# Moving three small operations of a threshold search from VectorE to GpSimd, and reordering ScalarE, in a sparse-attention block

## The chip, the cores and the metric

One core of one Trainium2 chip. The metric is the device time of one execution in microseconds, median of several. TensorE is PE in the profile's rows, VectorE is DVE, ScalarE is ACT, GpSimd is POOL.

## The reference, cut to what matters

A transformer block on x of shape (16, 512, 128): attention with 16 heads of 64 and 16 memory keys per head, whose scores are mixed across heads, cut to each row's 64 largest, and whose probabilities are mixed across heads again; then a gated feed-forward layer (384 hidden). Both are wrapped in layer norms and residuals.

```python
q, k, v = split_heads(x @ Wq), split_heads(x @ Wk), split_heads(x @ Wv)
k, v = concat([mem_k, k]), concat([mem_v, v])
dots = einsum('bhij,hk->bkij', einsum('bhid,bhjd->bhij', q, k) * scale, pre_proj)
dots = where(causal, neg, dots)
vk = top_k(dots, 64)[0][..., -1:]
attn = softmax(where(dots < vk, neg, dots))
out = einsum('bhij,bhjd->bhid', einsum('bhij,hk->bkij', attn, post_proj), v)
```

## The kernel before, in words

The weights are folded once at the start, so that a head's scores are one product of x' with a 128x512 matrix. Then come 16 batches of 16 heads: 256 heads, one **step** per head and a few steps to drain. Batches 1 to 14 run in a loop over b, two batches per turn, with the 16 steps written out. Each engine has its own program; they meet by semaphores alone. The 512 queries of a head stand as four tiles t of 128 rows with 144, 272, 400 and 528 columns (keys up to the diagonal and 16 memory keys); `ORDER` is 3, 2, 1, 0.

In step s the engines work on several heads at once, at lags of 0 to 7 steps:

- **Score** (lag 0): TensorE makes the scores (L760), VectorE copies them out with the row maximum (L1209). GpSimd places the memory scores (L1332) and, a step later, the negative maximum `negmax` (L1317).
- **Guess** (lags 1 to 3): the 64th largest score of each row is searched for. Three rounds, three heads at a time: ScalarE counts by a Sign activation with its sum (L915, twelve in a step) how many scores lie above a guess, and VectorE makes the next guess by a secant or bracket step out of a chain of small instructions, 12 or 24 columns wide, each of which waits for the one before: L1122 `miss`, L1123 `between`, L1127 `product`, L1130, L1134, L1138, L1140, L1142 (reciprocal), L1143, L1145, L1148 (the new guesses, `guess_ready`).
- **Select** (`LAG_K`, 4): VectorE counts the scores at or above the last guess (L1075, `count_found`, sum in `found`), GpSimd subtracts (L1357, four instructions), which hides them from the eight-largest search.
- **Check** (`LAG_E`, 5): VectorE tests (L1104 `spread`, L1109 `missed`) whether the count was within a window; TensorE adds the flags over the rows (L749, `raise_flag`), VectorE copies them out of PSUM between two L1209 (L1072, `copy_flag`). A missed tile gets a general search (L1042 to L1050). ScalarE makes the exponentials (L936).
- **Apply** (`LAG_P`, 6): VectorE takes the eight largest of the rest (L1089, four MAX8). GpSimd's `offset` (L1338) gives the rank that each would have, L1092 picks the one of rank 64 and L1097 adds it up to `kth`. Then VectorE masks and sums the probabilities (L1190, four) and takes the reciprocal `rinv` (L1195); GpSimd makes four diagonals of it (L1349) and `pmem` (L1363); TensorE turns and scales the blocks by them (L784), ScalarE takes them out of PSUM (L926).
- **Values** (`LAG_V`, 7): TensorE adds up the output (L771).

VectorE's order in a step: MAX8, L1092, L1097, L1104, L1109, the guess chain, L1075 of tile 3, a feed-forward pair (L1164, L1170; steps 11 to 13), L1075 of tile 2, L1190 four times, L1195, L1075 of tiles 1 and 0, L1209 four times. At its end stand the statistics of a norm (L1010, L1015; steps 0, 7, 8, 14) or the memory maxima (L1030, step 10).

GpSimd's order: negmax, seed copy (L1323), memory copy, offset, then in steps 1, 8, 9 and 15 a norm (L1258, L1261, L1265 for x, L1270) and in 8 and 15 a residual (L1276, L1277), the diagonals, the subtractions, pmem.

TensorE's order: scores, a piece of other work, weighing, the next head's matrix G, the flag, the turned blocks, other work. In step 7 the memory part of the output (L738) stands ahead of the weighing. ScalarE's order: counts, other copies, turned block 0, G (L846), block 1, exponential of tile 3, block 2, the other exponentials, other copies.

`alone` (L281) is a nop that carries an instruction's waits, so that the instruction itself has none.

## Time and profile before

| | us |
|---|---|
| median of 3 runs | 3318.77 (3317.39 to 3321.68) |
| the profiled execution | 3324.22 |
| its span, first to last instruction | 3322.4 |
| busy: VectorE | 2884.4 (87%) |
| ScalarE | 2882.6 (87%) |
| TensorE matmuls | 2794.6 (84%) |
| GpSimd | 1737.9 (52%) |

The granted TensorE clock is 0.954 of full speed on average. DMA is nearly idle: 7 GB/s. Busy time counts instructions of the engine and not its waits, nops and semaphore instructions; instructions of one engine may overlap by some 0.05 to 0.1 us, so that the start of one and the start of the next are what adds up. The profile's page gives shares over the whole span; for a change inside the step the timelines of a single step say more, and these are read below.

### The profile page before, as it was taken

How to read it: one execution, taken by the hardware profiler on the slowest of the kernel's cores; microseconds unless marked ns; L12 is line 12 of the kernel's file. 1: busy time of each engine (PE TensorE's matmuls, PEld its weight loads, DVE VectorE, ACT ScalarE, POOL GpSimd, SP SyncE). 2: the span in 40 equal slices, each digit the busy share in tenths (PEclk: the TensorE clock that was granted, in tenths of full speed). 3: DMA queues.
4: the chain of work that ended last, by engine and by line, in shares of the span. 5: the costliest groups of instructions: out<-in, count | busy, mean ns of one | idle time of the engine just before them, and what ended most of it. 6: DMA issues, size and time to landing. Idle time of an engine off the chain costs nothing. (4 is left out here: it accounts for less than half of the span.)

```text
span 3322.4 us, 76028 instructions
## 1 busy us (share of the span) xinstructions
PE 2794.6 (84%) x16314; PEld 2046.5 (62%) x16314; DVE 2884.4 (87%) x12547; ACT 2882.6 (87%) x8666; POOL 1737.9 (52%) x3623
## 2 busy tenths in 40 slices
PE   6888888888878888888898878888788898888865
PEld 3466666666656666666666656666566666666654
DVE  4599888989989899998889989989889889998884
ACT  1699899998978989899898979989899898989972
POOL 3355555555545555555555545545555555555543
PEclk9999999999989999999999989999999999999987
DMA  1000000000000000000000000000000000000000
GB/s 45 7 2 2 5 8 5 9 2 5 9 5 9 2 12 2 5 9 5 9 2 12 2 5 8 2 12 2 5 9 5 9 2 12 2 5 9 2 8 4
DMA packets 31421, 22.93 MB, mean 7 GB/s; under 512 B 3201, under 2 KB 30338, under 8 KB 30722
## 3 DMA queue, kind: packets, MB, share of 16 engines
q1 hardware_dynamic: 30722, 16.03, 1.7%
q14 instruction: 555, 4.55, 0.5%
q8 instruction: 144, 2.36, 0.3%
HBM read 11.83 MB, written 4.19 MB: 5 GB/s over the span
## 5 line engine op out<-in xcount | busy, mean ns | idle before, releaser
L915 ACT ACTIVATE signs<-scores,state 128x528 int8<-128x528 f32 (+3 forms) x3072 | 1726.3, 585 | 40.5 <-DVE state L1148 40.0
L784 PE MATMUL t_bank<-diag,probs 128*128 128x128 f32 x5120 | 760.9, 308 | 453.8 <-POOL diag L1349 400.5
L1349 POOL TENSOR_SCALAR diag<-ident,rinv 128x128 f32<-128x128 f32 x1024 | 362.2, 374 | 1360.1 <-DVE rinv L1195 1360.1
L784 PEld LDWEIGHTS t_bank<-diag,probs 128*128 128x128 f32 x5120 | 694.2, 216 | 494.1 <-issue 359.1
L1357 POOL TENSOR_TENSOR work<-scores,work 128x528 f32<-128x528 f32 (+3 forms) x1024 | 889.0, 903 | 10.8 <-DVE work L1075 10.8
L760 PE MATMUL s_bank<-xn,gT 128*128 128x512 f32 (+3 forms) x2048 | 685.7, 457 | 0.9 <-ACT gT L846 0.7
L771 PEld LDWEIGHTS y_bank<-u_all,probsT 128*128 128x128 f32 x5120 | 609.0, 192 | 107.3 <-issue 98.9
L915 ACT ACTIVATION_READ_ACCUMULATOR signs<-scores,state 128x1 f32 x3072 | 646.5, 210 | 0.0
L926 ACT COPY probsT<-t_bank 128x512 f32<-128x512 f32 (+1 forms) x768 | 406.9, 530 | 266.3 <-PE t_bank L784 265.1
L771 PE MATMUL y_bank<-u_all,probsT 128*128 128x128 f32 x5120 | 617.3, 276 | 5.3 <-ACT probsT L926 5.3
L1075 DVE TENSOR_SCALAR_CACHE_REDUCE work<-scores,state 128x528 f32<-128x528 f32 (+3 forms) x1024 | 531.1, 553 | 46.2 <-DVE state L1148 46.2
L936 ACT ACTIVATE expo<-scores,negmax 128x528 f32<-128x528 f32 (+3 forms) x1024 | 546.7, 599 | 0.0
L1190 DVE SCALAR_TENSOR_TENSOR probs<-scores,kth,expo 128x528 f32<-128x528 f32 (+3 forms) x1024 | 525.5, 569 | 12.3 <-ACT expo L936 5.8
L1209 DVE TENSOR_SCALAR_CACHE_REDUCE scores<-s_bank,memmax 128x512 f32<-128x512 f32 (+3 forms) x1024 | 516.7, 543 | 6.0 <-PE s_bank L762 6.0
L760 PEld LDWEIGHTS s_bank<-xn,gT 128*128 128x128 f32 x2048 | 326.5, 193 | 227.9 <-issue 220.5
L1089 DVE MAX8 state<-work 128x8 f32<-128x528 f32 (+3 forms) x1024 | 441.6, 491 | 0.2 <-issue 0.2
L632 PE MATMUL misc<-b_all,xn 128*128 128x512 f32 x512 | 273.4, 616 | 7.5 <-ACT u_all L846 7.5
L669 PE MATMUL misc<-xn,a_all 128*128 128x512 f32 x512 | 262.5, 594 | 0.0
L762 PE MATMUL s_bank<-causal,ident 128*128 128x128 bf16 x1024 | 224.6, 219 | 0.0
L762 PEld LDWEIGHTS s_bank<-causal,ident 128*128 128x128 bf16 x1024 | 101.1, 99 | 103.3 <-issue 63.2
L846 ACT COPY u_all<-misc 128x512 f32<-128x512 f32 x256 | 151.4, 591 | 7.0 <-PE misc L632 7.0
L846 ACT COPY gT<-misc 128x512 f32<-128x512 f32 x256 | 154.2, 602 | 0.9 <-PE misc L669 0.9
(156 smaller groups left out, 2846.5 us busy)
## 6 DMA issues: line engine op xcount, KB each, us to landing
xwork<-in_L_attn_x_dram SPq DMA_DIRECT2D x17, 256.0 KB, 2.8
xres<-in_L_attn_x_dram SPq DMA_DIRECT2D x16, 256.0 KB, 2.9
out_dram<-ybuf SPq DMA_DIRECT2D x16, 256.0 KB, 2.4
u_all<-in_L_attn_Wq_dram SPq DMA_DIRECT2D x1, 512.0 KB, 3.6
u_all<-in_L_attn_Wk_dram SPq DMA_DIRECT2D x1, 512.0 KB, 4.5
u_all<-in_L_attn_Wv_dram SPq DMA_DIRECT2D x1, 512.0 KB, 5.5
u_all<-in_L_attn_Wo_dram SPq DMA_DIRECT2D x1, 512.0 KB
expo<-in_L_ffn_w_gate_dram SPq DMA_DIRECT2D x1, 192.0 KB, 4.7
```

Of the source, the lines that this page charges most:

```text
L760: nc.tensor.matmul(score_part(t, 0, KEYS[t]), lhsT=gT[s % 2][:, t * P:(t + 1) * P], rhs=xn[par][:, 0:KEYS[t]], start=True, stop=False, ski ...
L771: mm = nc.tensor.matmul(y_bank[:, t * P:(t + 1) * P], lhsT=probsT[:, h % 2, at:at + P], rhs=u_all[:, j, h * D:(h + 1) * D], start=False, s ...
L784: mm = nc.tensor.matmul(t_bank[q % 2][:, at:at + P], lhsT=probs[:, h % 2, KEY_AT[t] + j * P:KEY_AT[t] + (j + 1) * P], rhs=diag[:, t, :], s ...
L915: nc.scalar.activation(signs[:, k, AT[t]:AT[t] + ROW[t]], row(scores, ring(head_of(s, k + 1), RING), t), ACT.Sign, bias=guesses(s % STATES ...
L926: nc.scalar.copy(probsT[:, h % 2, PART_AT[q]:PART_AT[q + 1]], t_bank[q % 2][:, 0:PART_AT[q + 1] - PART_AT[q]]).then_inc(t_taken, 1)
L936: nc.scalar.activation(row(expo, ring(head_of(s, LAG_E), ERING), t), row(scores, ring(head_of(s, LAG_E), RING), t), ACT.Exp, bias=negmax[: ...
L1075: v.tensor_scalar(work[:, s % 2, AT[t]:AT[t] + ROW[t]], row(scores, slot_k, t), guessed[:, t:t + 1], None, ALU.is_ge, ALU.add, accum_out=f ...
L1089: v.max(candidates(past)[:, t, 1:9], work[:, s % 2, AT[t]:AT[t] + ROW[t]]).then_inc(select_step, 1)
L1190: v.scalar_tensor_tensor(out=probs[:, slot_p % 2, AT[t]:AT[t] + ROW[t]], in0=row(scores, slot_p, t), scalar=kth[:, bass.ds(slot_p, 1), t], ...
L1209: v.tensor_scalar(keys(scores, slot, t), score_part(t, 0, KEYS[t]), 1.0, memmax[par][:, t, bass.ds(s, 1)], ALU.mult, ALU.max, accum_out=ro ...
L1349: nc.gpsimd.tensor_scalar(diag[:, t, :], ident[:, :], rinv[:, slot_p, t:t + 1], 1.0, ALU.mult, ALU.mult).then_inc(scaled, 1)
L1357: nc.gpsimd.tensor_tensor(wrk, row(scores, slot_k, t), wrk, ALU.subtract).then_inc(hidden, 1)
```

## The change

- **GpSimd tests missed rows, a step ahead.** The constants of L1338 get two more columns a tile, so that one addition of `found` gives the two distances from the window's ends too; `spread` is their product (a tensor_tensor of 128x4), `missed` a comparison (tensor_scalar). Both, and `offset`, now run at `LAG_K`, behind the diagonals and ahead of the subtractions. `offset` and `missed` get two buffers. VectorE's L1104 and L1109 go. The sum over the tiles, which L1109 made by its accumulator, is made by `copy_flag`, now a tensor_scalar with an accumulator.
- **TensorE** makes the flag right behind the scores, and no longer behind weighing and G.
- **`between` (L1123)** moves to GpSimd, a step ahead, behind the norms and ahead of the diagonals; it waits for the guess of its own step. VectorE's L1130 waits for it.
- **The pick** (L1092, L1097) moves from ahead of the guess chain into it: the rank weighing stands behind L1145, ahead of L1148, the sum behind L1148.
- **The count of tile 2** moves between the two feed-forward products L1164 and L1170.
- **ScalarE** takes G and the exponentials of tiles 3 and 2 ahead of turned block 0, then blocks 0 and 1, exponential 1, block 2, exponential 0.

```diff
@@ -137,11 +137,13 @@
             active = n + M > TOPK
             table[i, t] = z * UNIT ** 0.5
             table[i, T + t] = (z - FAR / (2 * density)) * UNIT ** 0.5
-            table[i, 5 * T + 9 * T + t] = float(active)
-            table[i, 5 * T + 10 * T + t] = 0.0 if active else -FMAX
+            reach = WINDOW + 0.5 if active else FAR
+            table[i, 5 * T + 11 * t] = reach - AIM
+            table[i, 5 * T + 11 * t + 1] = -reach - AIM
+            table[i, 5 * T + 11 * T + t] = 0.0 if active else -FMAX
         for k in range(GUESSES):
             table[:, 2 * T + k * T + t] = ROW[t] - 2 * AIM - 0.25
-        table[:, 5 * T + 9 * t:5 * T + 9 * t + 9] = np.arange(9) - TOPK
+        table[:, 5 * T + 11 * t + 2:5 * T + 11 * t + 11] = np.arange(9) - TOPK
     return table
 
 
...
@@ -791,6 +795,8 @@
                     g = b * H + s
                     if kind != "drain":
                         score(kind, b, par, s, g)
+                    if lagged(kind, s, LAG_E):
+                        raise_flag(kind, g - LAG_E, head_of(s, LAG_E) % 2)
                     make_extra(kind, b, par, s, 0)
                     if s == LAG_V and kind != "first":
                         memory_y(kind, b)
@@ -801,8 +807,6 @@
                         weigh(head_of(s, LAG_V), g - LAG_V)
                     if makes_g(kind, s):
                         product_g(kind, b, par, par if s < H - 1 else 1 - par, s + 1)
-                    if lagged(kind, s, LAG_E):
-                        raise_flag(kind, g - LAG_E)
                     if lagged(kind, s, LAG_P):
                         for q in range(3):
                             turn(head_of(s, LAG_P), g - LAG_P, q)
@@ -947,14 +951,15 @@
                     count(2)
                     count(1)
                     take_extra(0)
-                    take_turned(0)
                     if makes_g(kind, s):
                         take(kind, b, par, ("G", s + 1), gT[(s + 1) % 2][:, :])
+                    exponentials(0)
+                    exponentials(1)
+                    take_turned(0)
                     take_turned(1)
-                    exponentials(0)
+                    exponentials(2)
                     take_turned(2)
-                    for p in range(1, T):
-                        exponentials(p)
+                    exponentials(3)
                     take_extra(1)
 
                 for s in range(H):
@@ -1053,7 +1058,7 @@
 
             dve.wait_ge(table_in, 16)
             dve.wait_ge(state_set, 3)
-            nc.vector.tensor_copy(offset[:, :, 9:10].squeeze(2), cap)
+            nc.vector.tensor_copy(offset[:, :, :, 11:12].squeeze(3), cap.unsqueeze(1).to_broadcast([P, 2, T]))
 
             def batch(kind, b, par):
                 def step(s):
@@ -1069,12 +1074,26 @@
 
                         dve.wait_ge(flag_full, ge + 1)
                         alone(dve)
-                        v.tensor_copy(flags[:, :], flag_part).then_inc(flag_taken, 1)
+                        v.tensor_scalar(flags[:, 0:T], flag_part, 1.0, None, ALU.mult, ALU.add,
+                                        accum_out=flags[:, T:T + 1]).then_inc(flag_taken, 1)
 
                     def count_found(t):
                         v.tensor_scalar(work[:, s % 2, AT[t]:AT[t] + ROW[t]], row(scores, slot_k, t), guessed[:, t:t + 1],
                                         None, ALU.is_ge, ALU.add,
                                         accum_out=found[:, s % 2, t:t + 1]).then_inc(found_ready, 1)
+
+                    def weigh_ranks():
+                        dve.wait_ge(offset_ready, gp + 1)
+                        dve.wait_ge(select_step, T)
+                        v.scalar_tensor_tensor(out=offset[:, slot_p % 2, :, 2:11], in0=offset[:, slot_p % 2, :, 2:11], scalar=0.0,
+                                               in1=candidates(past), op0=ALU.is_equal,
+                                               op1=ALU.mult).then_inc(select_step, 1)
+
+                    def pick():
+                        dve.wait_ge(select_step, T + 1)
+                        dve.sem_clear(select_step)
+                        v.tensor_reduce(kth[:, bass.ds(slot_p, 1), :].squeeze(1), offset[:, slot_p % 2, :, 2:12], AX_X,
+                                        ALU.add).then_inc(kth_ready, 1)
 
                     if applies:
 
@@ -1087,28 +1106,6 @@
                                 rows_missed = dve.value_load(flags[0:1, T:T + 1].bitcast(I32), min_val=0,
                                                              max_val=2 ** 31 - 1)
                             v.max(candidates(past)[:, t, 1:9], work[:, s % 2, AT[t]:AT[t] + ROW[t]]).then_inc(select_step, 1)
-                        dve.wait_ge(offset_ready, gp + 1)
-                        dve.wait_ge(select_step, T + 1)
-                        v.scalar_tensor_tensor(out=offset[:, :, 0:9], in0=offset[:, :, 0:9], scalar=0.0,
-                                               in1=candidates(past), op0=ALU.is_equal,
-                                               op1=ALU.mult).then_inc(select_step, 1)
-                        dve.wait_ge(select_step, T + 2)
-                        dve.sem_clear(select_step)
-                        v.tensor_reduce(kth[:, bass.ds(slot_p, 1), :].squeeze(1), offset[:, :, :], AX_X,
-                                        ALU.add).then_inc(kth_ready, 1)
-
-                    if checks:
-                        number = found[:, (s - 1) % 2, :]
-                        dve.wait_ge(found_ready, 4 * ge + 4)
-                        alone(dve)
-                        v.scalar_tensor_tensor(out=spread[:, :], in0=number, scalar=-2.0 * AIM, in1=number,
-                                               op0=ALU.add, op1=ALU.mult).then_inc(select_step, 1)
-                        dve.wait_ge(select_step, 1)
-                        at_least(dve, flag_full, ge)
-                        alone(dve)
-                        v.scalar_tensor_tensor(out=missed[:, 0:T], in0=spread[:, :], scalar=WINDOW ** 2 + 0.5 - AIM ** 2,
-                                               in1=active, op0=ALU.is_gt, op1=ALU.mult,
-                                               accum_out=missed[:, T:T + 1]).then_inc(bad_ready, 1)
 
                     if moves:
                         for k in range(GUESSES):
@@ -1120,13 +1117,13 @@
                         miss = pair(last, S_T, 0)[:, 1]
                         both, last_at = last_and_now(last)
                         v.tensor_tensor(miss, counts[:, (s - 1) % 2, :], aim_sum, ALU.subtract).then_inc(guess_step, 1)
-                        v.tensor_tensor(between[:, :, :], pair(past, S_T, -1), pair(last, S_OTHER, 0),
-                                        ALU.subtract).then_inc(guess_step, 1)
                         dve.wait_ge(guess_step, 1)
 
                         v.tensor_tensor(product[:, :, :], both, miss.unsqueeze(1).to_broadcast([P, 2, ALL]),
                                         ALU.mult).then_inc(guess_step, 1)
-                        dve.wait_ge(guess_step, 3)
+                        dve.wait_ge(guess_step, 2)
+                        dve.wait_ge(between_ready, g - 1)
+                        alone(dve)
                         v.scalar_tensor_tensor(out=between[:, :, :],
                                                in0=product[:, last_at, :].unsqueeze(1).to_broadcast([P, 2, ALL]),
                                                scalar=0.0, in1=between[:, :, :], op0=ALU.is_lt,
@@ -1134,18 +1131,25 @@
                         v.scalar_tensor_tensor(out=move[:, :], in0=product[:, 1 - last_at, :],
                                                scalar=(2 * WINDOW + 0.25) ** 2 + 1.0,
                                                in1=miss, op0=ALU.is_gt, op1=ALU.mult).then_inc(guess_step, 1)
-                        dve.wait_ge(guess_step, 4)
+                        dve.wait_ge(guess_step, 3)
                         v.tensor_tensor(other, pair(last, S_OTHER, 0), between[:, :, :], ALU.add).then_inc(guess_step, 1)
+                        dve.wait_ge(guess_step, 5)
+                        v.tensor_tensor(apart[:, :, :], pair(last, S_T, 0), other, ALU.subtract).then_inc(guess_step, 1)
                         dve.wait_ge(guess_step, 6)
-                        v.tensor_tensor(apart[:, :, :], pair(last, S_T, 0), other, ALU.subtract).then_inc(guess_step, 1)
-                        dve.wait_ge(guess_step, 7)
                         v.reciprocal(apart[:, 1, :], apart[:, 1, :]).then_inc(guess_step, 1)
                         v.tensor_tensor(move[:, :], apart[:, 0, :], move[:, :], ALU.mult).then_inc(guess_step, 1)
+                        dve.wait_ge(guess_step, 8)
+                        v.tensor_tensor(move[:, :], move[:, :], apart[:, 1, :], ALU.mult).then_inc(guess_step, 1)
                         dve.wait_ge(guess_step, 9)
-                        v.tensor_tensor(move[:, :], move[:, :], apart[:, 1, :], ALU.mult).then_inc(guess_step, 1)
-                        dve.wait_ge(guess_step, 10)
                         dve.sem_clear(guess_step)
+                        if applies:
+                            weigh_ranks()
                         v.tensor_tensor(guesses(now, 1, GUESSES), guess, move[:, :], ALU.subtract).then_inc(guess_ready, 1)
+
+                    if applies:
+                        if not moves:
+                            weigh_ranks()
+                        pick()
 
                     if selects:
                         guessed = guesses(now, GUESSES, 1)
@@ -1164,13 +1168,15 @@
                         v.scalar_tensor_tensor(out=f_up[:, c, :], in0=f_tanh[:, c, :], scalar=1.0,
                                                in1=misc[gate_at][:, :], op0=ALU.add, op1=ALU.mult
                                                ).then_inc(misc_free[gate_at], 1)
+
+                    if selects:
+                        count_found(ORDER[1])
+
+                    if 11 <= s < 11 + HC and kind != "first":
                         dve.wait_ge(misc_free[gate_at], turns_of_bank(kind, b, misc_at(kind, ("GATE", c))) + 1)
                         dve.wait_ge(misc_full, misc_index(kind, b, ("UP", c)) + 1)
                         alone(dve)
                         v.tensor_tensor(f_up[:, c, :], f_up[:, c, :], misc[up_at][:, :], ALU.mult).then_inc(misc_free[up_at], 1)
-
-                    if selects:
-                        count_found(ORDER[1])
 
                     if applies:
                         at_least(dve, t_full, 3 * (gp - 1))
@@ -1331,14 +1337,14 @@
                         alone(pool)
                         nc.gpsimd.tensor_copy(mem_parts(scores[:, bass.ds(slot, 1), :].squeeze(1)),
                                               head_mem(smem[par], s)).then_inc(mem_placed, 1)
-                    if lagged(kind, s, LAG_E):
-                        at_least(pool, kth_ready, g - LAG_E)
-                        pool.wait_ge(found_ready, 4 * (g - LAG_E) + 4)
+                    extras(kind, b, s)
+                    moves_next = any(lagged(kind, s + 1, k + 2) for k in range(GUESSES)) if s + 1 < H else kind != "drain"
+                    if moves_next:
+                        at_least(pool, guess_ready, g - 1)
+                        at_least(pool, first_ready, g if kind != "drain" or s == 0 else 0)
                         alone(pool)
-                        nc.gpsimd.tensor_tensor(offset[:, :, 0:9], ranks,
-                                                found[:, (s - 1) % 2, :].unsqueeze(2).to_broadcast([P, T, 9]),
-                                                ALU.add).then_inc(offset_ready, 1)
-                    extras(kind, b, s)
+                        nc.gpsimd.tensor_tensor(between[:, :, :], pair((s - 1) % STATES, S_T, -1), pair(s % STATES, S_OTHER, 0),
+                                                ALU.subtract).then_inc(between_ready, 1)
                     gp, slot_p = g - LAG_P, head_of(s, LAG_P) % 2
                     if lagged(kind, s, LAG_P):
                         pool.wait_ge(rinv_ready, gp + 1)
@@ -1350,6 +1356,22 @@
                                                     ALU.mult).then_inc(scaled, 1)
                     if lagged(kind, s, LAG_K):
                         gk, slot_k = g - LAG_K, ring(head_of(s, LAG_K), RING)
+                        ranked = offset[:, slot_k % 2, :, :]
+                        at_least(pool, kth_ready, gk - 1)
+                        pool.wait_ge(found_ready, 4 * gk + 4)
+                        alone(pool)
+                        nc.gpsimd.tensor_tensor(ranked[:, :, 0:11], ranks,
+                                                found[:, s % 2, :].unsqueeze(2).to_broadcast([P, T, 11]),
+                                                ALU.add).then_inc(offset_ready, 1)
+                        pool.wait_ge(offset_ready, gk + 1)
+                        alone(pool)
+                        nc.gpsimd.tensor_tensor(spread[:, :], ranked[:, :, 0:1].squeeze(2), ranked[:, :, 1:2].squeeze(2),
+                                                ALU.mult).then_inc(spread_ready, 1)
+                        pool.wait_ge(spread_ready, gk + 1)
+                        at_least(pool, flag_full, gk - 1)
+                        alone(pool)
+                        nc.gpsimd.tensor_scalar(missed[:, slot_k % 2, :], spread[:, :], 0.0, 1.0, ALU.is_gt,
+                                                ALU.mult).then_inc(bad_ready, 1)
                         for p, t in enumerate(ORDER):
                             pool.wait_ge(found_ready, 4 * gk + p + 1)
                             alone(pool)
```

## Rows read from the trace of the kernel before

**Rows 1.** Windows: a plain step, then sixteen steps; us and instructions of each engine, clock, DMA.
```profile
core 0: us, PE busy (x) PEld busy (x) DVE busy (x) ACT busy (x) POOL busy (x), PEclk, DMA share, GB/s
1500.99:1512.05 11.06, 10.06 (x61) 7.13 (x60) 10.10 (x46) 11.06 (x35) 5.81 (x13) 1.00 0.00 1
1538.17:1733.60 195.43, 170.47 (x1008) 126.23 (x1007) 175.48 (x775) 179.08 (x541) 106.73 (x226) 0.96 0.02 6
```

**Rows 2.** Waits: who waited for whom; us in total, times, longest.
```profile
DVE flags L1072 <- issue: 20.4, 16, 2.6
...
DVE f_up L1170 <- DVE f_up L1164: 5.9, 30, 0.2
```

**Rows 3.** Timeline of VectorE in a plain step: start us, us, what.
```profile
1504.64 0.18 DVE L1195 RECIPROCAL rinv<-rowsum 128x4 f32<-128x4 f32 x1
...
1507.37 1.73 DVE L1089 MAX8 state<-work 128x8 f32<-128x528 f32 x4
1509.21 0.33 DVE L1092 SCALAR_TENSOR_TENSOR offset<-offset,state 128x36 f32<-128x36 f32 x1
...
1510.37 0.17 DVE L1122 TENSOR_TENSOR state<-counts,consts 128x12 f32<-128x12 f32 x1
...
1510.80 0.18 DVE L1130 SCALAR_TENSOR_TENSOR between<-product,between 128x24 f32<-128x24 f32 x1
...
1511.75 0.17 DVE L1145 TENSOR_TENSOR move<-move,apart 128x12 f32<-128x12 f32 x1
...
1512.39 0.76 DVE L1075 TENSOR_SCALAR_CACHE_REDUCE work<-scores,state 128x528 f32<-128x528 f32 x1 [0.17 <-DVE state L1148]
```

**Rows 4.** Timeline of GpSimd in the same step, asked in short windows.
```profile
1506.45 1.31 POOL L1357 TENSOR_TENSOR work<-scores,work 128x528 f32<-128x528 f32 x1
...
1507.71 1.04 POOL L1357 TENSOR_TENSOR work<-scores,work 128x400 f32<-128x400 f32 x1
...
1508.70 0.76 POOL L1357 TENSOR_TENSOR work<-scores,work 128x272 f32<-128x272 f32 x1
...
1509.42 0.49 POOL L1357 TENSOR_TENSOR work<-scores,work 128x144 f32<-128x144 f32 x1
1509.87 0.30 POOL L1363 TENSOR_TENSOR pmem<-probs,rinv 128x64 f32<-128x64 f32 x1
1510.12 0.21 POOL L1317 TENSOR_TENSOR negmax<-rowmax,minus_unit 128x4 f32<-128x4 f32 x1
...
1510.39 0.25 POOL L1332 COPY scores<-smem 128x64 f32<-128x64 f32 x1
```

**Rows 5.** Timeline of VectorE and GpSimd in one of the last steps.
```profile
3244.49 0.58 DVE L1109 SCALAR_TENSOR_TENSOR missed<-spread,consts 128x4 f32<-128x4 f32 x1
...
3245.01 0.53 DVE L1122 TENSOR_TENSOR state<-counts,consts 128x12 f32<-128x12 f32 x1
...
3242.04 3.47 POOL L1357 TENSOR_TENSOR work<-scores,work 128x528 f32<-128x528 f32 x4
```

**Rows 6.** Timeline of both engines while GpSimd normalises x (step 1).
```profile
1649.96 1.04 POOL L1261 TENSOR_TENSOR rstd<-vareps,minus_half 128x4 f32<-128x4 f32 x1
...
1650.23 0.18 DVE L1138 TENSOR_TENSOR state<-state,between 128x24 f32<-128x24 f32 x1
...
1651.14 1.04 POOL L1265 TENSOR_TENSOR xwork<-xwork,meanvar 128x512 f32<-128x512 f32 x1
1651.26 0.95 DVE L1148 TENSOR_TENSOR state<-state,move 128x12 f32<-128x12 f32 x1
```

**Rows 7.** Timeline of both engines while GpSimd adds the residual (step 8).
```profile
1539.75 0.96 DVE L1190 SCALAR_TENSOR_TENSOR probs<-scores,kth,expo 128x528 f32<-128x528 f32 x1
1540.10 1.19 POOL L1277 TENSOR_TENSOR xres<-xres,ybuf 128x256 f32<-128x256 f32 x1
...
1540.64 1.09 DVE L1190 SCALAR_TENSOR_TENSOR probs<-scores,kth,expo 128x400 f32<-128x400 f32 x1
```

**Rows 8.** Timeline of VectorE at the end of step 7.
```profile
1532.19 0.85 DVE L1010 BATCH_NORM_STATS2 stats<-ybuf 128x6 f32<-128x128 f32 x4
...
1533.47 1.71 DVE L1089 MAX8 state<-work 128x8 f32<-128x528 f32 x4
```

20 lines of the change are left out of this document (11 added, 9 removed).

## The prediction

> **What bounds the kernel now.** I read the windows first. In a plain step (one without norm statistics, maxima or feed-forward work on VectorE) ScalarE is busy for all of 11.06 us and VectorE for 10.10; over sixteen steps, 195.43 us, ScalarE has 16.4 us to spare, VectorE 19.9, GpSimd 88.7 [rows 1]. The timeline of VectorE then shows that its spare time is latency: it goes straight from one small dependent instruction to the next, and starts the next head's count when the guess is done [rows 3]. It hardly waits for others; the waits name a flag (20.4 us in 16 places) and the feed-forward products (5.9 us) [rows 2]. So VectorE's own chain sets the step, 12.2 us on average, and ScalarE with 179.08/16 = 11.2 us of work is the next limit, 1.0 us below.
>
> Times from here count from the end of L1195 (1504.82 in rows 3). MAX8 runs from 2.55 to 4.28 (four instructions; the next small one, L1092, starts at 4.39), L1122 at 5.55, L1130 at 5.98, L1145 at 6.93, the first count L1075 at 7.57 [rows 3]. GpSimd, which also starts from L1195, subtracts in four pieces from 1.63 to 5.10, then pmem to 5.35, negmax, seed and memory copy to 5.83 [rows 4]. Both orders hang on the same instruction, so their phase repeats in every step.
>
> **What is removed.** L1092 to L1122 is 1.16 us of rank weighing, sum, spread and missed; all leaves this place. L1123 was issued in the latency of L1122 and saves nothing. If nothing came in its way, L1122 would start at 4.25 (its waits are met, and it need not wait for MAX8's result), 1.3 us sooner.
>
> **What comes in.** L1130 gets a second wait and a nop, 0.1 us. Behind L1145 stand the rank weighing and, behind L1148, the sum: L1145 to L1075 is 0.64 us now [rows 3]; with up to 0.33 for the one and 0.2 for the other and their waits I take 1.0 (bounds 0.75 and 1.15). The flag's copy gets an accumulator read, which overlaps the next L1209: nothing, at most 0.1. Without other effects a step gains 1.3 - 0.1 - 0.36 = 0.85 us.
>
> **Where it collides.** GpSimd gets three small instructions between the diagonals and the subtractions. Their kind takes 0.21 to 0.25 us (negmax, the memory copy [rows 4]), and one that depends on the one before starts 0.14 behind its end (L1261 to L1265 [rows 6]): 0.25 + 0.14 + 0.21 + 0.14 + 0.23 = 0.97 us (bounds 0.7 and 1.1). The pieces now start at 2.60, 3.86, 4.85 and 5.57 and end at 3.91, 4.90, 5.61 and 6.06; pmem ends at 6.31, negmax at 6.47, the memory copy at 6.78. VectorE's guess chain has two operands in SBUF nearly throughout, and the rows show what happens to such an instruction under a GpSimd one: in the last steps L1122, 0.17 us in rows 3, took 0.53, and L1109 ahead of it 0.58; their ends, 3245.07 and 3245.54, are 0.02 to 0.03 behind the ends of the third piece and of the last one (3245.51) [rows 5]. L1148 took 0.95, to 0.03 behind the end of L1265 [rows 6]. GpSimd's pieces kept their pace.
>
> So in a plain step after the change: L1122 starts at 4.3 and ends with the second piece, 4.92; the product starts 0.04 later, under the third piece, ends 5.65; L1130 ends with the fourth, 6.10; L1134 with pmem, 6.35; L1138 with negmax, 6.51; L1140 with the memory copy, 6.82. L1142 follows at 6.86, L1145 at 7.15, L1075 at 8.15 against 7.57: **0.58 us slower**, where the free chain would be 0.85 faster. Five of sixteen steps are clean like this (+2.9 us); six more have waits of their own for instructions or registers that partly overlap the block; I estimate +0.25 each, between nothing and 0.58 (+1.5 us).
>
> In five steps VectorE does 1.1 to 1.3 us of other work ahead of MAX8 (L1010 to the next MAX8 is 1.28 [rows 8]). MAX8 then ends near 5.55 and only the product meets a full piece. L1075 starts at about 8.2. Before it was 5.55 + 3.29 = 8.84, and in four of the five (steps 1, 8, 9, 15; 52 times in the trace, all like the one shown) L1148 was caught by a norm's pass, 0.95 for 0.17, another 0.78 [rows 6]: 9.6. These passes now start at about 8.33, and L1148 at 7.75, so it is through. Gains 1.3 at steps 9, 15, 1.1 at 1 and 0.4 at 11. Step 8 gains 1.3 and also 1.1 of the flag's wait, as TensorE makes the flag ahead of the long weighing and not behind it: 20.4/16 = 1.28 [rows 2]. But L1190 comes earlier into GpSimd's residual and centring passes: the engines then take turns, as they do in some steps now, L1190 0.96 and then, with fewer elements, 1.09, and L1277 1.19 [rows 7]. Each turn costs VectorE what is left of a pass, 0.2 to 0.6. I charge 0.8 at steps 1, 8 and 15 (bounds 0 and 1.2), less 0.3 at 8, where every second batch pays it now. Net for steps 9, 15, 1, 8, 11: -1.3 - 0.5 - 0.3 - 1.9 - 0.4 = -4.4 us.
>
> A count between the two feed-forward products hides their 0.1 us latency and wait, three times: -0.4 us. **ScalarE's new order** I cost at nothing: it fills waits with work, but nobody waits for ScalarE; what covers it is VectorE's 12.2 us step, and if that fell under 11.2 it would be worth what ScalarE idles. GpSimd's `between` runs beside L1075, which has one SBUF operand, and is due 8 us later: nothing; if GpSimd were late there, the diagonals behind it would be.
>
> **Sum.** 2.9 + 1.5 - 4.4 - 0.4 = -0.4 us in sixteen steps, 16 batches: -6. The profiled execution took 3324.2 (span 3322.4), so 3318; the median shown is 5.4 lower, so **3312 us**. The gain from the shorter chain is real and is eaten by the collision.
>
> One row decides a further term. L1261 ran from 1649.96 to 1651.00, and L1138 inside it took 0.18, as L1130 does alone [rows 3, 6], so I let the power instruction block nobody. If it did block, as L1265 does, L1145 would wait for its end in four steps of a batch and its successors would meet the norm behind it: 0.8 + 0.8 = 1.6 us each, 16 x 4 x 1.6 = 100 us, 3412. The Trainium skill (SBUF — State Buffer, Who interferes with whom) says that a VectorE instruction with two SBUF inputs and a GpSimd one that reads SBUF exclude each other for the whole instruction, which would be this case; the trace agrees for the subtractions and norms, and disagrees for L1261.
>
> **Rivals.**
> 1. The chain is hardly caught (my phase is wrong, or the first small instruction slips in and the rest follow). Each step gains 0.85, plus the L1148 blocks and the flag: 16 x 0.85 + 4 x 0.78 + 1.3 = 18 us in a batch; ScalarE's work (179.08 us a batch [rows 1]) and its remaining waits cap that at 8 to 12: 3125 to 3190 us. Against it: no instruction slipped through [rows 5]. For it: the phase is put together from small durations. 0.15.
> 2. **Slower:** the late steps gain less than I count. If L1148 starts later than 8.3 (0.5 behind my 7.75), the norm's pass catches it again: 0.78 in four steps, 3.1 us a batch; with 0.58 in all eleven plain steps instead of seven's worth (another 2.0), +4.7 us a batch, 3394 us. It decides from a chain 0.5 us longer than mine, or a GpSimd shift of 0.7 or less that brings the norms forward. For it: the margins are a few tenths. 0.2.
> 3. The power instruction blocks too, as worked out above, 3412 us: L1138 speaks against it [rows 6]. 0.03.
> 4. The forecast, 3312, within 3270 to 3355: 0.62. It is the difference of two terms of 70 and 77 us, so its sign is open: about half of it is faster, a fifth within 0.2% (7 us, about what a measurement of this kernel can tell from no change), the rest slower.
>
> Faster: 0.15 + 0.31 = 0.46; same 0.12; slower 0.2 + 0.03 + 0.19 = 0.42. The range leaves out rivals 1 and 3 and little more: 3220 to 3395.
>
> **What would show it.** In a plain step: L1122, the product, L1130, L1134 of 0.3 to 0.7 us each, ending 0.02 to 0.04 behind L1357's pieces and pmem, and L1075 8.15 behind L1195 (rival 1: 6.7). The first L1357 at 2.6. L1148's longest duration: 0.17 as I say, 0.95 for rival 2. No wait in front of the flag's copy at step 7. L1190 and L1277 stretched at 1, 8 and 15. ScalarE's wait for turned blocks nearly gone, without a gain in time. I am wrong if VectorE's small instructions keep 0.17 us while the subtractions run, or if VectorE waits for ScalarE's counts.

## The result, and the profile of the changed kernel

The changed kernel takes **3371.24 us** (median of 4 runs, 3367.18 to 3372.79) against 3320.11 for the kernel before: ratio 1.0152, 95% interval 1.0136 to 1.0168. It is slower by 51 us, where I forecast 3312. One run of the woven version in experiment 6 took 5454.96 us against 3241 to 3248 of its other three, which alone have a median of 3242.86; its median, ratio and interval below count that run. The profiled execution has a span of 3365.2 us at a mean granted clock of 0.962; the one before had 3322.4.

The windows of a plain step and of sixteen steps, with the columns of [rows 1]:

```profile
1528.34:1539.96 11.62, 10.20 (x63) 7.21 (x62) 11.01 (x45) 11.45 (x35) 6.45 (x16) 1.00 0.01 2
1565.37:1761.74 196.37, 169.82 (x1005) 123.54 (x1006) 183.37 (x729) 180.14 (x537) 119.21 (x273) 0.97 0.02 6
```

VectorE is busy for 11.01 of 11.62 us where it was for 10.10 of 11.06, with one instruction fewer (45 for 46). So its instructions got longer. The timeline of VectorE in a plain step, which answers to [rows 3]:

```profile
1909.53 0.18 DVE L1201 RECIPROCAL rinv<-rowsum 128x4 f32<-128x4 f32 x1
...
1912.27 1.73 DVE L1108 MAX8 state<-work 128x8 f32<-128x528 f32 x4
1913.92 0.74 DVE L1119 TENSOR_TENSOR state<-counts,consts 128x12 f32<-128x12 f32 x1
1914.69 0.69 DVE L1122 TENSOR_TENSOR product<-state 128x24 f32<-128x24 f32 x1
1915.52 0.31 DVE L1127 SCALAR_TENSOR_TENSOR between<-product,between 128x24 f32<-128x24 f32 x1
1915.76 0.32 DVE L1131 SCALAR_TENSOR_TENSOR move<-product,state 128x12 f32<-128x12 f32 x1
1915.99 0.24 DVE L1135 TENSOR_TENSOR state<-state,between 128x24 f32<-128x24 f32 x1
1916.27 0.27 DVE L1137 TENSOR_TENSOR apart<-state 128x24 f32<-128x24 f32 x1
...
1916.86 0.17 DVE L1142 TENSOR_TENSOR move<-move,apart 128x12 f32<-128x12 f32 x1
1917.24 0.22 DVE L1088 SCALAR_TENSOR_TENSOR offset<-offset,state 128x36 f32<-128x36 f32 x1 [0.21 <-DVE move L1142]
1917.38 0.17 DVE L1147 TENSOR_TENSOR state<-state,move 128x12 f32<-128x12 f32 x1
1917.60 0.20 DVE L1095 TENSOR_REDUCE kth<-offset 128x4 f32<-128x40 f32 x1
1917.83 0.76 DVE L1081 TENSOR_SCALAR_CACHE_REDUCE work<-scores,state 128x528 f32<-128x528 f32 x1
```

and GpSimd in the same step, which answers to [rows 4] (a row now holds the four pieces):

```profile
1911.34 0.26 POOL L1363 TENSOR_TENSOR offset<-consts,found 128x44 f32<-128x44 f32 x1
1911.74 0.20 POOL L1368 TENSOR_TENSOR spread<-offset 128x4 f32<-128x4 f32 x1
1912.13 0.24 POOL L1373 TENSOR_SCALAR missed<-spread 128x4 f32<-128x4 f32 x1 [0.19 <-POOL spread L1368]
1912.33 3.46 POOL L1379 TENSOR_TENSOR work<-scores,work 128x528 f32<-128x528 f32 x4
1915.75 0.29 POOL L1385 TENSOR_TENSOR pmem<-probs,rinv 128x64 f32<-128x64 f32 x1
1916.00 0.20 POOL L1323 TENSOR_TENSOR negmax<-rowmax,minus_unit 128x4 f32<-128x4 f32 x1
...
1916.27 0.24 POOL L1338 COPY scores<-smem 128x64 f32<-128x64 f32 x1
```

Count again from the reciprocal's end, 1909.71. The three tests take 1911.34 to 1912.33, so the subtractions start at 2.62 instead of 1.63 and end at 6.08. The first small instruction behind MAX8 (L1119) starts at 4.21 and takes 0.74 us, the product 0.69. The next four end at 1915.83, 1916.08, 1916.23 and 1916.54, and GpSimd's last piece, pmem, negmax and memory copy at 1915.79, 1916.04, 1916.20 and 1916.51: each is held to 0.03 or 0.04 us behind one of them. The first count (L1081) starts at 8.12; it was 7.57.

The waits of VectorE, which answer to [rows 2]:

```profile
DVE offset L1088 <- DVE move L1142: 60.9, 254, 0.6
DVE probs L1196 <- issue: 33.7, 46, 3.5
...
DVE f_up L1179 <- PE misc L732: 0.4, 1, 0.4
```

The flag (20.4 us before) and the latency of the feed-forward products (5.9) are gone, as forecast. A wait of "issue" in front of `probs` is new: 33.7 us in 46 places. Before it was 5.6 in 3: 3.5 us in a step that ran the general search, 1.9 where the loop ends and 0.2 at the end of the program. It is the second half of the story. In step 9 of every second batch:

```profile
1967.24 0.76 DVE L1081 TENSOR_SCALAR_CACHE_REDUCE work<-scores,state 128x528 f32<-128x528 f32 x1
...
1967.93 0.63 DVE L1081 TENSOR_SCALAR_CACHE_REDUCE work<-scores,state 128x400 f32<-128x400 f32 x1
...
1969.41 0.77 DVE L1196 SCALAR_TENSOR_TENSOR probs<-scores,kth,expo 128x528 f32<-128x528 f32 x1 [0.85 <-issue]
```

ScalarE had ended the exponentials of that head 6 us earlier:

```profile
1962.66 0.42 ACT L940 ACTIVATE expo<-scores,negmax 128x144 f32<-128x144 f32 x1
```

Between the second count and `probs` VectorE's sequencer passes a conditional branch (L1187, in the kernel before L1181), past the general search for rows whose candidates don't suffice. In most steps the next instruction of the sequencer follows the branch 0.51 us later, which the second count covers; in four places of the loop's 32 steps (steps 7 and 9 of one batch, 4 and 15 of the other), 1.2 to 1.8 us later. In a fifth, step 0, that instruction is in time and `probs` behind it is late.

I split steps 16 to 255 of both traces at four instructions; after less before, sums in us: reciprocal to the end of MAX8 -18.6; MAX8 to the first count +8.4 (plain steps +76, the five long ones -68); first count to `probs` +21.0; `probs` to the reciprocal +29.9. Together +40.8. The long steps are 1, 8, 9, 11 and 15, in which VectorE does other work ahead of MAX8.

The last section holds the turns that the prediction names: VectorE's L1196 and GpSimd's residual hold each other up, at steps 1, 8 and 15. In step 8 (400 columns take 0.63 us in a plain step):

```profile
1562.89 1.09 DVE L1196 SCALAR_TENSOR_TENSOR probs<-scores,kth,expo 128x400 f32<-128x400 f32 x1
```

```profile
1562.27 1.27 POOL L1282 TENSOR_TENSOR xres<-xres,ybuf 128x256 f32<-128x256 f32 x1
```

### The profile page after: what moved, and what is told of

Same layout as the page of the kernel before. It is cut to its first block and busy times, and to the rows that moved or that the text cites. A ratio compares the mean times of both kernels' runs of the same rounds, so it can differ in the third digit from the quotient of the medians.

```text
span 3365.2 us, 76754 instructions
## 1 busy us (share of the span) xinstructions
PE 2815.9 (84%) x16314; PEld 2023.6 (60%) x16314; DVE 3015.9 (90%) x11777; ACT 2912.6 (87%) x8666; POOL 1937.2 (58%) x4393
## 5 line engine op out<-in xcount | busy, mean ns | idle before, releaser
L788 PE MATMUL t_bank<-diag,probs 128*128 128x128 f32 x5120 | 746.9, 301 | 476.6 <-POOL diag L1355 372.5
L788 PEld LDWEIGHTS t_bank<-diag,probs 128*128 128x128 f32 x5120 | 671.5, 208 | 702.7 <-issue 525.3
L1196 DVE SCALAR_TENSOR_TENSOR probs<-scores,kth,expo 128x528 f32<-128x528 f32 (+3 forms) x1024 | 555.2, 597 | 39.4 <-issue 33.4
L919 ACT ACTIVATION_READ_ACCUMULATOR signs<-scores,state 128x1 f32 x3072 | 581.8, 189 | 0.0
L940 ACT ACTIVATE expo<-scores,negmax 128x528 f32<-128x528 f32 (+3 forms) x1024 | 564.5, 577 | 0.0
L1081 DVE TENSOR_SCALAR_CACHE_REDUCE work<-scores,state 128x528 f32<-128x528 f32 (+3 forms) x1024 | 531.1, 553 | 16.4 <-issue 3.6
L930 ACT COPY probsT<-t_bank 128x512 f32<-128x512 f32 (+1 forms) x768 | 376.3, 510 | 179.6 <-PE t_bank L788 177.7
L636 PE MATMUL misc<-b_all,xn 128*128 128x512 f32 x512 | 281.1, 631 | 7.5 <-ACT u_all L850 7.5
L1346 POOL TENSOR_TENSOR between<-state 128x24 f32<-128x24 f32 x258 | 74.5, 289 | 262.1 <-DVE state L1147 262.1
L1122 DVE TENSOR_TENSOR product<-state 128x24 f32<-128x24 f32 x258 | 157.1, 609 | 9.0 <-DVE state L1119 0.2
```

Of the source, the lines that this page charges most:

```text
L788: mm = nc.tensor.matmul(t_bank[q % 2][:, at:at + P], lhsT=probs[:, h % 2, KEY_AT[t] + j * P:KEY_AT[t] + (j + 1) * P], rhs=diag[:, t, :], s ...
L919: nc.scalar.activation(signs[:, k, AT[t]:AT[t] + ROW[t]], row(scores, ring(head_of(s, k + 1), RING), t), ACT.Sign, bias=guesses(s % STATES ...
L930: nc.scalar.copy(probsT[:, h % 2, PART_AT[q]:PART_AT[q + 1]], t_bank[q % 2][:, 0:PART_AT[q + 1] - PART_AT[q]]).then_inc(t_taken, 1)
L940: nc.scalar.activation(row(expo, ring(head_of(s, LAG_E), ERING), t), row(scores, ring(head_of(s, LAG_E), RING), t), ACT.Exp, bias=negmax[: ...
L1081: v.tensor_scalar(work[:, s % 2, AT[t]:AT[t] + ROW[t]], row(scores, slot_k, t), guessed[:, t:t + 1], None, ALU.is_ge, ALU.add, accum_out=f ...
L1196: v.scalar_tensor_tensor(out=probs[:, slot_p % 2, AT[t]:AT[t] + ROW[t]], in0=row(scores, slot_p, t), scalar=kth[:, bass.ds(slot_p, 1), t], ...
```

## The experiments

The kernel before took 3319 to 3324 us (medians) beside them. Ratios are to it, with their intervals.

**1. The flag alone**, in the kernel before:

```diff
                         score(kind, b, par, s, g)
+                    if lagged(kind, s, LAG_E):
+                        raise_flag(kind, g - LAG_E)
                     make_extra(kind, b, par, s, 0)
...
-                    if lagged(kind, s, LAG_E):
-                        raise_flag(kind, g - LAG_E)
```

> The kernel before, with only TensorE's flag product moved to right behind the scores. If the wait of VectorE in front of the flag's copy at step 7 (20.4 us in 16 places before, none after the change) is on the path, this alone gives the 18.6 us that the section from L1195 to the end of MAX8 gained in the changed kernel: 3300 us, ratio 0.994. Rival: the wait only moves (to the statistics behind it or to ScalarE's counts): ratio 1.000.

3304.81 us, 0.994 (0.9923 to 0.9956). The section ahead of MAX8's end loses 21.0 us, 19.6 of it at step 8. The flag is worth what the prediction gave it.

**2. ScalarE's order alone**, in the kernel before (the order of the diff above, nothing else):

> The kernel before, with only ScalarE's new order. As VectorE's chain sets the step and waits for ScalarE hardly anywhere, I expect ratio 1.000 within 0.001 and ScalarE's wait for turned blocks much reduced. Rival: ScalarE's order brings its exponentials of tiles 1 and 0 later or its counts earlier, and shows in the time: ratio 0.99 or 1.01.

3345.08 us, 1.0067 (1.005 to 1.0084), **not** nothing. The wait for the flag has grown from 20.4 us [rows 2] to 45.2; the row of that kernel's waits:

```profile
DVE flags L1073 <- issue: 45.2, 18, 5.2
```

**3. Both together**, in the kernel before, if the order costs only through the late flag:

> The kernel before with two parts of the change, the flag's matmul right behind the scores and ScalarE's new order. Theory (ScalarE's order cost 22 us alone because it made TensorE's late flag later still; with the early flag nobody waits for it): 0.994 of the kernel before, the same as the early flag alone, 3300 to 3310 us. Rival (the order costs VectorE something by itself): 1.000 or above.

3310.79 us, 0.9974 (0.9964 to 0.9984): between the two. Of the 20.7 us that the order cost ahead of MAX8's end, 1.7 are left, as the theory has it, so the two parts are not independent. But the time is just above my range. What stays, 0.0034 or about 11 us over the flag alone, is nearly all another wait, again for TensorE, in the feed-forward steps (8.1 us at step 11). In the kernel before it was 4.6 us, with the flag alone 6.7; with the flag and the order:

```profile
DVE f_up L1171 <- PE misc L728: 18.0, 24, 1.4
```

**4. The changed kernel with the old order of ScalarE:**

> The changed kernel with ScalarE's order of the kernel before. Theory (as in the prediction, the order is hidden in this kernel: VectorE waits 0.4 us in all for the UP product): 3365 to 3377 us, the same as the changed kernel. Rival (the order costs here too, as it did alone): 3340 to 3360 us.

3378.1 us, 1.0182 (1.0166 to 1.0198), 1 us above my range and 7 us above the changed kernel's 1.0152. There the new order is free, even of some use; VectorE waits 0.4 us in all for that product.

**5. The subtractions taken away** from the changed kernel:

```diff
-  nc.gpsimd.tensor_tensor(wrk, row(scores, slot_k, t), wrk, ALU.subtract).then_inc(hidden, 1)
+  nc.gpsimd.tensor_tensor(wrk[:, 0:1], row(scores, slot_k, t)[:, 0:1], wrk[:, 0:1],
+                          ALU.subtract).then_inc(hidden, 1)
...
-  v.max(candidates(past)[:, t, 1:9], work[:, s % 2, AT[t]:AT[t] + ROW[t]]).then_inc(select_step, 1)
+  v.max(candidates(past)[:, t, 1:9], row(scores, slot_p, t)).then_inc(select_step, 1)
```

It leaves out the hiding of the keys above the guess (one column is still subtracted), and MAX8 reads the scores as they are.

> The changed kernel with GpSimd's four subtractions cut to one column each, and MAX8 reading the scores themselves, so that it does as much work as ever; left out is the hiding of the scores above the guess, so the threshold is another one. Collision theory: with the subtractions gone VectorE's guess chain runs freely, L1122, product, L1130 and L1134 fall to 0.17 to 0.2 us, L1075 starts near 6.8 instead of 8.13 behind L1195, and ScalarE (11.2 us a step) becomes the limit: 3150 to 3230 us. Rival (the chain's own latency and instruction supply make the loss): 3340 or more.

3233.02 us, 0.9733 (0.9717 to 0.9749), 138 us under the changed kernel and 3 us above my range. The chain in a step without other work of VectorE:

```profile
1824.16 1.73 DVE L1108 MAX8 state<-scores 128x8 f32<-128x528 f32 x4
1826.79 0.17 DVE L1119 TENSOR_TENSOR state<-counts,consts 128x12 f32<-128x12 f32 x1 [0.90 <-issue]
1826.99 0.18 DVE L1122 TENSOR_TENSOR product<-state 128x24 f32<-128x24 f32 x1
1827.32 0.18 DVE L1127 SCALAR_TENSOR_TENSOR between<-product,between 128x24 f32<-128x24 f32 x1
1827.42 0.17 DVE L1131 SCALAR_TENSOR_TENSOR move<-product,state 128x12 f32<-128x12 f32 x1
1827.54 0.18 DVE L1135 TENSOR_TENSOR state<-state,between 128x24 f32<-128x24 f32 x1
```

Every small instruction is at its own length. In plain steps where nothing else is waited for, the first count starts at 6.61 to 6.70 behind the reciprocal, the 6.7 of rival 1. But with VectorE this fast L1119 waits in steps 5 to 8 for ScalarE's counts (0.90 us here; the last count ended at 1826.70), and in steps 1, 8 and 15 the norm's passes now lie over the update, so that the first count comes at 9.2 to 10.4 (means of the steps). That is why not every step gains 1.5 us.

**6. The tests a step later.** GpSimd's three tests stand behind the memory copy, outside the stretch of the subtractions; once with the pick whole, ahead of the guess update, once woven in as in the change:

```diff
                         nc.gpsimd.tensor_copy(mem_parts(...), head_mem(smem[par], s)).then_inc(mem_placed, 1)
+                    if lagged(kind, s, LAG_E):
+                        ge = g - LAG_E
...
+                        nc.gpsimd.tensor_tensor(ranked[:, :, 0:11], ranks, ...).then_inc(offset_ready, 1)
...
+                        nc.gpsimd.tensor_tensor(spread[:, :], ...).then_inc(spread_ready, 1)
...
+                        nc.gpsimd.tensor_scalar(missed[:, par_e, :], ...).then_inc(bad_ready, 1)
                     extras(kind, b, s)
```

> The changed kernel, with GpSimd's three tests (offset, spread, missed) done a step later, behind the memory copy and so outside the subtractions' time, and the pick whole again, ahead of the guess update. Theory (the cost of the change is the later start of the subtractions, which then lie over the guess update): the first subtraction starts 1.63 us behind the reciprocal again, the first count of the next head 7.1 us behind it in a plain step (8.13 after the change, 7.57 before), 0.9 to 1.1 us less than after the change in eleven steps; 3215 to 3260 us, faster than both kernels. Rival (the weaving, or ScalarE's order, costs the time, or work moved anywhere on GpSimd costs VectorE as much): within 10 us of the changed kernel or above it.

> The same placing of GpSimd's tests, with the pick woven into the guess update as in the change. Theory: the product and its neighbours meet the subtractions' last piece, one instruction of latency is saved by the weaving; first count at 7.2 to 7.3 us, 3220 to 3270 us, within 15 us of the unwoven one. Rival (weaving is worth most of the gain, or costs it): the two differ by over 25 us.

Unwoven 3264.47 us, 0.9837 (0.9817 to 0.9856), 4 us above my range; its first count is at 7.4 in most plain steps, 0.7 us ahead of the changed kernel's, where I expected 0.9 to 1.1. Woven 3245.18 us, 0.9778 (0.9758 to 0.9797). The two differ by 19 us, 22 without the long run, which is neither my theory (within 15) nor the rival (over 25). A step of the woven one:

```profile
1837.22 0.48 DVE L1119 TENSOR_TENSOR state<-counts,consts 128x12 f32<-128x12 f32 x1
1837.73 0.43 DVE L1122 TENSOR_TENSOR product<-state 128x24 f32<-128x24 f32 x1
1838.30 0.19 DVE L1127 SCALAR_TENSOR_TENSOR between<-product,between 128x24 f32<-128x24 f32 x1
...
1840.30 0.76 DVE L1081 TENSOR_SCALAR_CACHE_REDUCE work<-scores,state 128x528 f32<-128x528 f32 x1
```

Counted from its reciprocal (1833.01), the first count is at 7.29, 0.83 ahead of the changed kernel's 8.12. That is 12 to 14 us over the trace for each of the eleven plain steps of a batch, and 124 us in the span. **One microsecond of phase on GpSimd decides the sign of this change.** The three instructions cost GpSimd the same in both versions; only what they push differs.

**7. The changed kernel with the pick unwoven** (tests where the change puts them):

```diff
+                        weigh_ranks()
+                        pick()
                     if moves:
...
-                        if applies:
-                            weigh_ranks()
...
-                    if applies:
-                        if not moves:
-                            weigh_ranks()
-                        pick()
```

> The changed kernel with the pick whole again, ahead of the guess update, and GpSimd's tests where the change puts them. Theory (in plain steps the guess update is paced by the subtractions' ends in either order, so the pick is hidden when it stands ahead, and lies bare behind the update when woven in): first count 0.2 to 0.3 us earlier in plain steps, 0.3 later in the five long ones; 3335 to 3365 us. Rival (the pick adds its whole length ahead of the update): 3385 us or above.

3328.74 us, 1.0035 (1.0022 to 1.0048), 42 us under the changed kernel and below my range.

```profile
1887.88 0.60 DVE L1088 SCALAR_TENSOR_TENSOR offset<-offset,state 128x36 f32<-128x36 f32 x1
1888.61 0.20 DVE L1095 TENSOR_REDUCE kth<-offset 128x4 f32<-128x40 f32 x1
1888.84 0.30 DVE L1121 TENSOR_TENSOR state<-counts,consts 128x12 f32<-128x12 f32 x1
1889.18 0.42 DVE L1124 TENSOR_TENSOR product<-state 128x24 f32<-128x24 f32 x1
...
1890.69 0.17 DVE L1144 TENSOR_TENSOR move<-move,apart 128x12 f32<-128x12 f32 x1
...
1891.33 0.76 DVE L1081 TENSOR_SCALAR_CACHE_REDUCE work<-scores,state 128x528 f32<-128x528 f32 x1 [0.16 <-DVE state L1147]
```

From its reciprocal (1883.48) the last `move` ends at 7.38; in the changed kernel it ends at 7.32 (1917.03 - 1909.71). So moving the pick away from in front of the update made the update only 0.06 us earlier: the time was filled by waiting for the subtractions. But behind it the pick lies bare, and the first count comes at 7.85 here and at 8.12 there. In the long steps, where MAX8 ends at 5.56 and little is left of the subtractions, the woven order is the better one, by 0.3 us in steps 1, 8 and 9, 0.15 in step 15 and nothing in 11. With the early subtractions of experiment 6 weaving gains 19 us; under the late ones it costs 42.

**8. The branch.** The changed kernel without the conditional block; it leaves out the general search:

```diff
-                        with dve.If(rows_missed > 0):
-                            for t in range(T):
...
-                                    general_kth(slot_p, t)
                         dve.wait_ge(exp_ready, 4 * gp + 4)
```

> The changed kernel without the conditional block behind the second count (the general search for rows whose candidates did not suffice, left out; the data do not need it). In the changed kernel VectorE stands 0.65 to 0.95 us longer behind this branch in steps 0 and 9 of every second batch, 7 and 4, 28 us in all, with its exponentials long done. Theory (the branch itself is what is waited for): these stalls go, 30 to 60 us less than the changed kernel, as every step also loses the branch's own time. Rival (it is a wait for data or for a count held elsewhere): the stalls stay, at most 15 us less.

3277.3 us, 0.9876 (0.986 to 0.9893), 94 us less, more than my 30 to 60. My text is wrong in one thing: the search does run with these data, four times in an execution (in the kernel before as well). A view of the changed kernel by the search's first line:

```profile
L1047 DVE COPY probs<-scores x4: 236/434/435, 948.2 to 3270.5; 128x528 f32<-128x528 f32 x3, 128x144 f32<-128x144 f32 x1
```

Three of them lie in the steps I compare, where they held VectorE for 15.8, 9.7 and 15.8 us; the fourth lies behind the last batch and held it for 15 us more. Without the four, some 38 us of the 94 are the branch's. The section from the first count to `probs` loses 80.2 us; less these 41.3, 38.9 us remain. Step 0 gives back 9.3 us, step 9 6.9, step 15 5.1, step 4 4.6, step 7 (beyond its two searches) 4.4, together 30.3: the stalls are gone, so it is the branch that was waited for. Nearly all the rest is some 0.17 us in each of the three feed-forward steps, 45 times.

**9. What picks the places?** Two tries to move them, both on the changed kernel: 32 empty instructions on VectorE ahead of the loop, and 12 within it, in step 3 of every second batch.

> The changed kernel with 32 nops on VectorE ahead of the loop, nothing else. In the changed kernel VectorE stands still for 0.6 to 0.9 us between the second L1081 and the first L1196 in steps 0, 7 and 9 of one batch of the pair and step 4 of the other, right behind the branch over the general search, with everything it waits for long done: about 28 us in all. If that is instruction supply, it hangs on where the code lies: the steps in which it falls change, and the time moves by up to 25 us either way. Rival: it is a wait for another engine, then the steps and the time stay as they are (ratio to the changed kernel 1.000).

> The changed kernel with 12 empty instructions on VectorE inside the loop, in step 3 of every second batch. In the changed kernel the instruction behind the branch follows it 0.51 us later in most steps, but 1.2 to 1.8 us later in steps 7 and 9 of even batches and 4 and 15 of odd ones. Theory (the slow places are set by where the branch lies in the loop's code): behind the added instructions the slow places move to other steps. Rival (they are set by what else the step does, transfers or other engines): the same steps are slow. The time is within 15 us of the changed kernel in either case.

3374.5 us, 1.0155 (1.0138 to 1.0172), and 3371.47 us, 1.0163 (1.0148 to 1.0179): the changed kernel's time, and the same steps stall by as much. **But neither edit changed the code that ran.** The empty instructions carry no wait, and the traces have none of them: VectorE has 17972 records in the changed kernel and in both of these. At the place of the twelve its sequencer's next three records start 0.04, 0.11 and 0.20 us behind the start of L1095, in the changed kernel and here; twelve instructions would not fit in between. So the two runs are repeats of the changed kernel, and neither theory nor rival was tested.

What the stalls are can be read from the trace itself. The profile's page also counts packets that fetch instructions; in the changed kernel, and without the conditional block (experiment 8):

```profile
q14 instruction: 574, 4.70, 0.5%
```

```profile
q14 instruction: 336, 2.75, 0.3%
```

Each of these packets is of 8192 bytes, but for a few at the start. In the slow place shown above (step 9) the branch stands at 1967.69; such a packet starts at 1967.53, and the sequencer goes on at 1969.34, 1.81 us behind the packet's start. At the four slow places there are 27 jumps in the steps compared (one more ran a search). In all of them a packet starts between 0.47 us ahead of the branch and 0.12 behind it, and the sequencer goes on 1.79 to 2.02 us behind its start, median 1.81. Of the 196 other jumps only 15 have one between 1 us ahead and 0.15 behind, on a queue whose engine the trace does not name. In step 0 `probs` starts 1.7 to 1.8 us behind such a packet. So **the long stalls are waits for instructions**. This rests on the traces alone; my reading is that the jump lands on code that is still to be fetched, behind a fetch that has just begun.

Two other traces fit. With late tests and the pick whole (experiment 6) the same places take 0.8 to 1.1 us, and the packet starts that much sooner; the distance from its start is 1.81 in the median again. Without the subtractions (experiment 5) the sequencer also goes on late in steps 5 and 6, but there it waits for ScalarE, until 0.04 us behind the end of the fourth exponential. In the kernel before, no jump within the loop takes over 0.75 us. That the places are set by where the blocks of fetched code end is a likely reading, which no run here tests: it takes an edit that moves the code.

**10. The best version:** late tests, woven pick, ScalarE's old order.

> The version with late tests and the woven pick (3245 us), with ScalarE's order of the kernel before. Theory (in the feed-forward steps VectorE's second product now waits 21.3 us for TensorE's UP product, 4.6 us in the kernel before, because ScalarE takes the turned blocks later): that wait falls to 5 us or less and the kernel to 3222 to 3235 us, ratio 0.971 to 0.975. Rival (the wait comes from VectorE being earlier, whatever ScalarE's order): within 6 us of 3245 us, and the wait stays above 15 us.

**3211.85 us, 0.9679 (0.9666 to 0.9692)**, 10 us under my range: 3.2% faster than the kernel before and 4.7% faster than the changed one. Experiment 6's wait for the UP product, and this kernel's:

```profile
DVE f_up L1179 <- PE misc L732: 21.3, 15, 1.9
```

```profile
DVE f_up L1178 <- PE misc L732: 2.5, 5, 0.7
```

Of the 31 us between the spans 26.0 are at step 11, where the wait stood, and 5.4 at step 8. ScalarE's new order was free in the changed kernel and costs 31 to 33 us (1%) in the faster one.

## Why the prediction was wrong

By its own steps:

1. *The subtractions start at 2.60, end at 6.06.* Measured 2.62 and 6.08. Right.
2. *The update is caught, L1075 at 8.15, +0.58 in a clean plain step.* Measured 8.12 or 8.13 in steps 5, 6 and 13, but 8.28 and 8.33 in 7 and 4, and experiment 5 gives the free chain's 6.6 to 6.7. Right in the main, and instruction by instruction: L1119 with the second piece, the product with the third, the next four with the last piece, pmem, negmax and the memory copy.
3. *L1148 escapes the norm's pass.* Right: 0.17 in all steps. But in step 9 it starts only 0.30 us ahead of the pass, where I counted 0.58:

```profile
1966.87 0.17 DVE L1147 TENSOR_TENSOR state<-state,move 128x12 f32<-128x12 f32 x1 [0.20 <-issue]
...
1967.17 1.04 POOL L1276 TENSOR_TENSOR xwork<-xres,rstd 128x512 f32<-128x512 f32 x1
```

4. *The flag's wait goes, 1.1 us in a batch; the turns cost 0.8 at steps 1, 8 and 15, less 0.3; f_up gains 0.4.* In 15 batches that is 16.5, 31.5 and 6 us; measured 18.6, 29.9 and 6.6. Right.
5. *Six other plain steps +0.25 each; five long steps gain.* This step failed by the size of its terms. The chain part of the eleven plain steps cost 76 us where the sum had 66 (4.4 us by 15 batches): the six that I put at 0.25 measured 0.35 on average. The five long steps' part gained 68 where it had 81 (the -4.4 of the sum, less the 2.1 of turns and the 1.1 of the flag, is -5.4 a batch). Their first count starts at 8.31 to 8.50 (means of the steps), not 8.2. **Here are 23 us of the miss**: the difference of two large terms, each about 15% off, and both to the slow side.
6. **What failed altogether is what was not in the sum:** the branch. I priced every instruction up to the first count and every one from `probs` on, and took the stretch between them for fixed. It grew by 21.0 us net, 28 of stalls less the 6.6 of f_up. The stalls are waits for instructions behind a jump (experiments 8 and 9). Nothing in the rows of before priced them, since no jump in its loop stalled; that changed code can bring such stalls was a term that I put at nothing without a reason.

So 23 + 28 us, less 4 for the small differences of the flag, the turns and f_up, is what stands between -6 and +40.8; the 2 us that the spans have more lie outside the steps compared. The collision was as forecast; the sign was decided by terms of 1%. The time lies within 3220 to 3395, but outside the 3270 to 3355 that I gave 0.62. It was partly luck that the wide range held it: the 28 us of stalls were in none of its cases.

*ScalarE's order costs nothing* was right for the changed kernel (experiment 4), where it even gains 7 us, and wrong as an argument: "nobody waits for ScalarE" overlooked TensorE, which waits for it in order and holds the flag (experiment 2) and the UP product (3, 10) behind its wait.

Rival 1 is what happens without the subtractions. Rival 2 had the place right (less gain in late steps) and the mechanism wrong, since L1148 was not caught. Rival 3 is refuted: the power instruction L1267 ran 1965.99 to 1967.03 at step 9, and L1142 (0.17) and L1147 (0.17) within it were not stretched.

```profile
1965.99 1.04 POOL L1267 TENSOR_TENSOR rstd<-vareps,minus_half 128x4 f32<-128x4 f32 x1
```

```profile
1966.06 0.17 DVE L1142 TENSOR_TENSOR move<-move,apart 128x12 f32<-128x12 f32 x1
```

## To carry to other kernels

Work moved to an idle engine is not free when it stands ahead of that engine's long passes: ask what it pushes, and onto which instructions of the other engine. Here the change with 1 us of small work ahead of the subtractions costs 51 us; with the same work behind them it gains 74 (76 without the long run), and 108 with ScalarE's order left alone. And an order is right or wrong only together with the others: the flag changed what ScalarE's order cost, and the phase of GpSimd changed the sign of the weaving. And before a run with added empty instructions is read, look in its trace whether they are there: here they were not.

## What the runs showed of the hardware

- A small VectorE instruction with two operands in SBUF is held to 0.03 or 0.04 us behind the end of the GpSimd instruction it meets, also when that one is small (pmem 0.29 us, negmax 0.20, the copy 0.24). L1095, with one operand, keeps its 0.20 us under the third piece in experiment 7, and the power instruction (1.04 us) did not stretch L1142 and L1147 (0.17 each) within it. The Trainium skill (SBUF — State Buffer, Who interferes with whom) has two such instructions exclude each other for the whole instruction; the trace agrees for the subtractions, pmem, negmax, the memory copy and the norm's passes, and disagrees for the power instruction.
- A branch that jumps over a block costs VectorE's sequencer 0.51 us in most places and 1.2 to 1.8 us in a few fixed ones of the changed kernel, where a packet of instructions starts just ahead of it; the sequencer goes on about 1.81 us behind that packet's start. The queued second count (0.63 us) covers the short wait and not the long one.
